# An early fetch of the first four tiles, an early split of the first weights, and all one-hot rows on VectorE

## The reference, cut to what matters

```python
logits = xf @ gate_w + gate_b
top_val, top_idx = jax.lax.top_k(logits, 2)
gate_score = jax.nn.softmax(top_val, axis=-1)
...
h = jax.nn.gelu(xf @ w1 + b1, approximate=False)
out = out + (h @ w2 + b2) * w[:, None]        # for each of the 8 experts
```

## Time and profile before

| what | value |
|---|---|
| time, median of 3 runs | 334.94 us (334.84 to 337.4) |
| time of the profiled execution | 337.69 us |
| its span in the profile | 336.0 us |
| busy: PE / PEld / DVE / ACT / POOL | 265.2 / 247.2 / 210.0 / 168.6 / 169.0 us |
| PE MATMUL L566 (fc1), x1872 | 154.5 us |
| PE MATMUL L582 (fc2), x936 | 150.7 us |
| POOL L1246 (one-hot rows), x32 | 32.0 us, mean 1010 ns |
| DVE L1130 (weights_lo), x16 | 36.7 us, mean 2293 ns |
| ACT L718 (weights_hi), x16 | 30.6 us, mean 1911 ns |
| chain that ended last | DMA 52%, issue 16%, PE 12%, DVE 9%, POOL 3%, ACT 3% |

### The profile page before, as it was taken

One profiled execution on the slowest core, in us unless ns is written; L12 is line 12 of the kernel. 1 busy time (PEld: TensorE's weight loads), 2 busy tenths in 40 slices (PEclk: granted clock), 3 DMA queues, 4 the chain that ended last, 5 costly groups with the idle time before them and its releaser, 6 DMA issues.

```text
span 336.0 us, 9465 instructions
## 1 busy us (share of the span) xinstructions
PE 265.2 (79%) x3109; PEld 247.2 (74%) x3109; DVE 210.0 (63%) x635; ACT 168.6 (50%) x465; POOL 169.0 (50%) x134
## 2 busy tenths in 40 slices
PE   3999952423014999999999999999999999999930
PEld 3998842312014989989999999998999999989920
DVE  5996689888963776766567656675575444443400
ACT  2042582463042886566756676567554544444410
POOL 5211106878952066666475657475636645463430
PEclk9985555555555999999999999999999999999995
DMA  6999999621114124454444444344434473435220
GB/s 183 352 375 377 376 376 375 234 95 64 64 44 100 19 34 70 77 90 72 82 69 79 67 80 75 73 69 77 78 69 67 80 97 66 77 58 78 28 22 14
DMA packets 47696, 40.17 MB, mean 120 GB/s; under 512 B 24113, under 2 KB 44354, under 8 KB 47650
## 3 DMA queue, kind: packets, MB, share of 16 engines
q1 hardware_dynamic: 39520, 28.85, 29.1%
q0 software_dynamic: 7488, 10.39, 20.3%
q10 hardware_dynamic: 642, 0.33, 0.4%
HBM read 25.07 MB, written 9.37 MB: 103 GB/s over the span
## 4 chain that ended last, share of the span: by engine, by line
DMA 52%; issue 16%; PE 12%; DVE 9%; POOL 3%; ACT 3%; DVEq 0%; ACTq 0%; POOLq 0%
DMA out_dram<-xn,add_at 50%; PE bank L421 4%; POOL wreg L1246 3%; PE bank L407 2%; DMA xs<-in_x_dram 1%; ACT wreg L718 1%; ACT xn L695 1%; DVE rows L944 1%; PE bank L449 1%; DVE wreg L1130 1%; DVE earlier L984 1%; PE bank L440 1%; DVE xs L921 1%; PE bank L485 1%; PE bank L464 1%
## 5 line engine op out<-in xcount | busy, mean ns | idle before, releaser
L566 PE MATMUL bank<-xTp,wreg 128*128 128x128 f16 x1872 | 154.5, 221 | 12.8 <-DVE wreg L1130 10.3
L582 PE MATMUL bank<-wreg,rows 128*128 x936 | 150.7, 273 | 0.0
L566 PEld LDWEIGHTS bank<-xTp,wreg 128*128 x1872 | 130.3, 99 | 21.8 <-issue 14.8
L782 ACT ACTIVATE rows<-bank,maskbias 128x128 f32<-128x128 f32 x312 | 88.6, 367 | 85.9 <-PE bank L566 36.5
L1274 POOL DMA_INDIRECT out_dram<-xn,add_at x39 | 78.4, 2011 | 92.1 <-ACT xn L792 61.1
L582 PEld LDWEIGHTS bank<-wreg,rows 128*128 128x128 f16 x936 | 80.7, 98 | 4.3
L1196 DVE TENSOR_SCALAR rows<-rows 128x512 f16<-128x512 f32 x78 | 33.8, 433 | 65.3 <-ACT rows L782 65.3
L1198 DVE SCALAR_TENSOR_TENSOR rows<-rows 128x512 f16<-128x512 f32 x78 | 54.0, 692 | 2.7
L1266 POOL DMA_INDIRECT xs<-xrows,fetch_at x39 | 45.4, 1165 | 18.0 <-issue 11.3
L1130 DVE SCALAR_TENSOR_TENSOR wreg<-wreg x16 | 36.7, 2293 | 19.7 <-ACT wreg L718 16.7
L718 ACT ACTIVATE wreg<-wreg x16 | 30.6, 1911 | 18.2 <-issue 14.5
(11 more groups left out here) (184 smaller groups left out, 209.8 us busy)
## 6 DMA issues: line engine op xcount, KB each, us to landing
wreg<-in_L_ffn_fc_w_dram SPq DMA_DIRECT2D x16, 1024.0 KB, 12.7
xrows<-rows SPq DMA_DIRECT2D x4, 528.0 KB, 3.0
xs<-in_x_dram SPq DMA_DIRECT2D x4, 512.0 KB, 8.5
out_dram<-xs SPq DMA_DIRECT2D x4, 512.0 KB, 8.6
xs<-xrows,fetch_at POOLq DMA_INDIRECT x39
xTp<-xs SPq DMA_TRANSPOSE x39
out_dram<-xn,add_at POOLq DMA_INDIRECT x39, 4.4
ctx_sb<-in_ctx_dram SPq DMA_DIRECT2D x1, 512.0 KB, 8.4
```

Source lines behind the costliest of these rows:

```text
L566: mm = pe.matmul(put, w, xT[:, i % NX, x_part, k, :], start=(k == 0 and n == 0), stop=(k == KC - 1 and n == 2))
L582: mm = pe.matmul(yb, h, w, start=False, stop=(c == FC - 1 and n == 2))
L782: op = act.activation(h32[i % 2][:, f * P:(f + 1) * P], bank[2 * (i % 2) + half][:, c * P:(c + 1) * P], ACT.Gelu, bias=b1cur[:, i % NX, f: ...
```

## The change

What it does, part by part:

1. One-hot rows: `at_col` and `at_rank` are both made on VectorE, as 16 `tensor_scalar` operations of 128 columns for each group, from an fp16 copy of the iota. GpSimd makes none. The rows move out of the spare weight region: one buffer of their own for groups 0 to 2, and a part of `xn` for group 3.
2. `row_low(3)` stands ahead of `slots(3)`; `norm1(3)` moves behind `add_attention(0)`.
3. `weights_hi(0)` waits on ACT for `units_ready` and the loads, and no longer for the token table. The cast of the token table moves from VectorE to ACT, behind `weights_hi(0)`.
4. The first expert always has four tiles; their columns, expert and regions are computed by themselves right behind `table_units` (`first_tiles`), PE makes a first fetch matmul from them, and VectorE copies the rows (`first_fetch`). Then come `weights_lo(0)`, `table_tiles`, `fetch(0)`, `weights_lo(1)` and `table_adds`.
5. PE makes a second fetch matmul ahead of the main loop. For tiles 0 to 3 it loads three registers from small tables; it waits for the full table at tile 4. It waits for unit 2r ahead of fc1 and for unit 2r+1 ahead of fc2 of an expert's first tile.

The diff, cut to its core:

```diff
-        spare = whalf[:, NU, :].rearrange("p (a b j q) -> p a b j q", a=2, b=2, j=GT * 2)
-        at_rank, at_col = spare[:, 0, :, :, :], spare[:, 1, :, :, :]
+        last_rows = xn[:, (NG - 2) % 2, :, :].rearrange("p t d -> p (t d)").bitcast(F16).rearrange("p (a j q) -> p a j q", a=2, j=GT * 2)
+        at_rank = [sb("at_rank", [P, GT * 2, P], F16)] * (NG - 1) + [last_rows[:, 0, :, :]]
+        at_col = [sb("at_col", [P, GT * 2, P], F16)] * (NG - 1) + [last_rows[:, 1, :, :]]
...
             pe.wait_ge(tokens_sb, 1)
             pe.wait_ge(cols_ready, 1)
-            pe.matmul(bank[0][:, 0:TILES], tokens_at[:, :], is_col[:, :], start=True, stop=True).then_inc(fetch_ps, 1)
-
-            pe.wait_ge(table_ready, 1)
-            pe.wait_ge(fetch_ready, 1)
+            pe.matmul(bank[6][:, 0:PER_RANK], tokens_at[:, :], is_col[:, 0:PER_RANK], start=True, stop=True).then_inc(fetch_ps, 1)
+            pe.wait_ge(cols_ready, 2)
+            pe.matmul(bank[6][:, 0:TILES], tokens_at[:, :], is_col[:, :], start=True, stop=True).then_inc(fetch_ps, 1)
+
...
                 if c == 0:
                     pe.wait_ge(xT_in[i % NX], (i // NX + 1) * 16)
+                    if i == 0 or unit_for(i) != unit_for(i - 1):
+                        pe.wait_ge(w_lo, unit_for(i) + 1)
...
+                if c == 0 and (i == 0 or unit_for(i) != unit_for(i - 1)):
+                    pe.wait_ge(w_lo, unit_for(i) + 2)
...
             def regions(i, n):
+                if i == 0:
+                    pe.wait_ge(first_ready, 1)
...
+                    return [(at[0], at[1], e) for j in range(n)]
+                if i == PER_RANK:
+                    pe.wait_ge(table_ready, 1)
...
+            weights_hi(0, unit_regions(0))
             act.wait_ge(tokens_ps, NG)
-            weights_hi(0, unit_regions(0))
+            act.activation(tokens_at[:, :], bank[1][:, 0:P], ACT.Copy).then_inc(tokens_sb, 1)
             at = unit_regions(1)
...
-                v.tensor_tensor(at_rank[:, g % 2, :, :], iota[:, :].unsqueeze(1).to_broadcast([P, GT * 2, P]),
-                                place_f[:, g, 1, :].unsqueeze(2).to_broadcast([P, GT * 2, P]),
-                                ALU.is_equal).then_inc(at_rank_ready, 1)
+
+            def onehot_rows(g):
+                if 1 <= g < NG - 1:
+                    v.wait_ge(tokens_ps, g)
+                if g == NG - 1:
+                    v.wait_ge(row_ready, g)
+                for j in range(GT * 2):
+                    n = g * GT + j // 2
+                    v.tensor_scalar(at_rank[g][:, j, :], iota_h[:, :], place_f[:, g, 1, j:j + 1], None, ALU.is_equal)
+                    op = v.tensor_scalar(at_col[g][:, j, :], iota_h[:, :], place_f[:, g, 0, j:j + 1], token[:, n:n + 1],
+                                         ALU.is_equal, ALU.mult)
+                op.then_inc(onehots, 1)
...
+            def first_tiles():
+                v.tensor_scalar(col_first[:, :], order_f[:, 0:1], float(RANKS // 2), None, ALU.mult).then_inc(vec_step, 1)
+                v.tensor_scalar(te_first[:, :], order_f[0:1, 0:1], 0.5, None, ALU.mult).then_inc(vec_step, 1)
+                v.tensor_copy(tw_first[:, 1:2], order_f[0:1, 0:1]).then_inc(vec_step, 1)
+                v.wait_ge(vec_step, done.up(3))
+                v.sem_inc(first_ready, 1)
+                v.tensor_scalar(is_col[:, 0:PER_RANK], iota_t[:, 0:PER_RANK], col_first[:, 0:1], iota_p[:, 0:1],
+                                ALU.add, ALU.is_equal).then_inc(cols_ready, 1)
+
+            def first_fetch():
+                v.wait_ge(fetch_ps, 1)
+                v.tensor_copy(fetch_at[:, 0:PER_RANK], bank[6][:, 0:PER_RANK]).then_inc(fetch_ready, 1)
...
             shift(3)
             route(3)
+            row_low(3)
             slots(3)
-            row_low(3)
+            onehot_rows(3)
             table_units()
+            first_tiles()
+            first_fetch()
+            weights_lo(0, unit_regions(0))
             table_tiles()
-            weights_lo(0, unit_regions(0))
-            table_adds()
-            weights_lo(1, unit_regions(1))
...
             fetch(0)
+            weights_lo(1, unit_regions(1))
+            table_adds()
             for i in range(TILES):
...
-            def onehot_rows(g):
-                pool.wait_ge(slots_ready, g + 1)
...
-                    op = pool.tensor_scalar(at_col[:, g % 2, j, :], iota[:, :], place_f[:, g, 0, j:j + 1], token[:, n:n + 1],
-                                            ALU.is_equal, ALU.mult)
-                op.then_inc(onehots, 1)
```

More of the change, by code:

```diff
@@ L61, in flamingo_block @@
     assert KC == 2 and HALVES == 2 and D == 256 and NG == 4 and FC == 8 and TILES == 39
-    assert GT == 2 * HALVES and 2 * NS == P and B == 2 * NG and NU < CODE and E * RANKS == P
+    assert GT == 2 * HALVES and 2 * NS == P and B == 2 * NG and NU < CODE and NXG == PER_RANK and (2 * T // E - 1) // P + 1 >= PER_RANK and E * RANKS == P
     xt = x.rearrange("b (h p) d -> p (b h) d", p=P)
@@ L125, in flamingo_block @@
         iota64 = iota[:, 0:NS]
+        iota_h = sb("iota_h", [P, P], F16)
         token = sb("token", [P, NT])
@@ L220, in flamingo_block @@
         te_i = sb("te_i", [1, TILES], I32)
+        te_first = sb("te_first", [1, 1], I32)
+        tw_first = sb("tw_first", [1, 2], I32)
+        col_first = sb("col_first", [P, 1])
         tw_i = sb("tw_i", [1, TILES, 2], I32)
@@ L310, in flamingo_block @@
         cols_ready = sem("cols_ready")
+        first_ready = sem("first_ready")
         fetch_ps = sem("fetch_ps")
@@ L336, in flamingo_block, with unit_for @@
             units_of_tile[(r - 1) * PER_RANK] = (2 * r + 1,)
-        def units_for(i):
-            return min(2 * (i // PER_RANK + 1), NU)
+        def unit_for(i):
+            return min(2 * (i // PER_RANK), NU - 2)
         block = stack.enter_context(nc.Block())
@@ L525, in token_table @@
                 pe.wait_ge(onehots, g + 1)
-                pe.wait_ge(at_rank_ready, g + 1)
                 for j in range(GT * 2):
-                    mm = pe.matmul(bank[1][:, 0:P], at_col[:, g % 2, j, :], at_rank[:, g % 2, j, :],
+                    mm = pe.matmul(bank[1][:, 0:P], at_col[g][:, j, :], at_rank[g][:, j, :],
                                    start=(g == 0 and j == 0), stop=(g == NG - 1 and j == GT * 2 - 1))
@@ L586, in regions @@
             def regions(i, n):
+                if i == 0:
+                    pe.wait_ge(first_ready, 1)
+                    at = nc.values_load_multi_w_load_instructions(
+                        tw_first[0:1, :], engines=[mybir.EngineType.PE], min_val=0, max_val=NU,
+                        skip_runtime_bounds_check_because="regions NU and 2e + 1 of an expert")[1]
+                    e = nc.values_load_multi_w_load_instructions(
+                        te_first[0:1, :], engines=[mybir.EngineType.PE], min_val=0, max_val=E - 1,
+                        skip_runtime_bounds_check_because="an expert")[1][0]
+                    return [(at[0], at[1], e) for j in range(n)]
+                if i == PER_RANK:
+                    pe.wait_ge(table_ready, 1)
                 at = nc.values_load_multi_w_load_instructions(
@@ L828, in _ @@
             v.memset(units_i[:, 0:1], NU).then_inc(vec_step, 1)
+            v.memset(tw_first[:, 0:1], NU).then_inc(vec_step, 1)
             v.wait_ge(pool_const, 2)
             v.tensor_copy(iota[:, :], iota_i[:, :]).then_inc(vec_step, 1)
+            v.tensor_copy(iota_h[:, :], iota_i[:, :]).then_inc(vec_step, 1)
             v.tensor_copy(token[:, :], iota_ki[:, :]).then_inc(vec_step, 1)
@@ L1108, in table_tiles @@
                 v.tensor_single_scalar(te_i[:, :], code_i[:, :], 5, op=ALU.logical_shift_right).then_inc(vec_step, 1)
-                v.wait_ge(fetch_ps, 1)
-                v.tensor_copy(fetch_at[:, :], bank[0][:, 0:TILES]).then_inc(fetch_ready, 1)
+                v.wait_ge(fetch_ps, 2)
+                v.tensor_copy(fetch_at[:, PER_RANK:TILES], bank[6][:, PER_RANK:TILES]).then_inc(fetch_ready, 1)
                 v.wait_ge(vec_step, done.up(2))
@@ L1138, in _ @@
             pick_sets(1)
-            norm1(3)
             weigh_sets(1)
             add_attention(0)
+            norm1(3)
             pick_sets(2)
@@ L1152, in _ @@
             slots(0)
+            onehot_rows(0)
             row_low(0)
@@ L1160, in _ @@
             slots(1)
+            onehot_rows(1)
             row_low(1)
@@ L1170, in _ @@
             slots(2)
+            onehot_rows(2)
             row_low(2)
@@ L1282, in _ @@
                 fetch_rows(i)
+            pool.wait_ge(fetch_ready, 2)
             pool.wait_ge(add_at_ready, 1)
```

18 lines of the change are left out of this document (3 added, 15 removed).

## The result

| | time, median of 4 runs (range) | profiled execution | its span |
|---|---|---|---|
| before | 334.94 us (334.84 to 337.4) | 337.69 us | 336.0 us |
| after | 341.24 us (338.7 to 342.21) | 342.21 us | 340.2 us |

The ratio of after to before is 1.0163, interval 1.011 to 1.0216: slower, by 3.7 to 7.2 us. Medians, here and in the experiments, are of all runs; the ratios leave out the few runs that the record marks as slow. The forecast was 339.0 us, +4.1 on the median before (a ratio of 1.012), in a range of 333.5 to 342.8.

What follows compares the result with a forecast made beforehand. PE was taken to bound the 39 tiles, so only its entry into the loop counts: PE's start +3.7 us, first fc2 +4.1, never taken back. Added to the median before, that gave 339.0 us, range 333.5 to 342.8.

Steps and rivals of the forecast that it cites:

- What bounds it: Main loop: PE bounds the 39 tiles, waiting only 2.5 us, so what decides is when PE gets in.
- Part 1, the pitch: One-hot rows on VectorE: 0.18 us each start to start, bounds 0.13 and 0.24; +5.19 over three groups.
- The credit for GpSimd's silence: Groups 1 to 3 on VectorE: without GpSimd's rows disturbing it, VectorE gains 1.25 us.
- Part 2: Moves: row_low(3) fills a 0.8 us wait and pushes slots(3) back 0.4; norm1(3) costs nothing, 0.2 at most.
- Part 3, ACT's order: ACT before first_fetch: the token table's cast stands behind weights_hi(0), so the early fetch is 3 us late, at 97.9.
- Part 4, the queue behind the new wait: VectorE stands still 3.4 us in first_fetch, its remaining list behind it; PE starts at 108.7, +3.7; fc2 at 115.3, +4.1.
- in the same cold clock: PE between first fc1 and fc2: the 72 matmuls take 6.19 us as before, reaching fc2 at 114.9.
- the 0.4 that I had for the split: First fc2: PE is there at 114.9 but waits for VectorE's split, so fc2 starts at 115.3.
- Cheap rows: Rival at the 64 one-hot operations: issued every 0.08 to 0.11 us; 333.9 us at 0.10, down to 331.2; chance 0.18.
- Dear rows: Rival at the one-hot rows: pitch 0.23 to 0.25 us, shift +7.3 to +8.6, 342.2 to 343.5 us; chance 0.15.
- The loop takes it back: Rival in the main loop: slack in GpSimd's output adds eats half the shift, 337.0 us; chance 0.1.
- The early start is one: Rival at first_fetch: ACT's cast slips ahead or VectorE's wait is short; 3.4 us less, +0.7, 335.6 us; chance 0.07.

Runs made afterwards that it cites:

- fp32_rows: Kernel after with its one-hot rows made from the fp32 iota instead of the fp16 copy; 344.5 us in one execution.
- norm_back: Kernel after with norm1(3) put back ahead of weigh_sets(1); 341.27 us, ratio 1.0112 to the kernel before.
- rows_only: Kernel before with only the one-hot rows moved to VectorE from the fp16 iota, in the old two buffers; 343.15 us, ratio 1.0128.
- cast_first: Kernel after with ACT's cast of the token table ahead of weights_hi(0); 339.21 us, ratio 1.0055 to the kernel before.
- tables_first: Kernel after with ACT's cast ahead of weights_hi(0) and table_tiles ahead of weights_lo(0); 338.68 us in one execution.
- early_start: cols_and_cast with PE's second fetch behind tile 0, table_tiles behind fetch(0), remaining tables behind tile 0's splits, and earlier register loads; 332.85 us, ratio 0.9886.
- cols_and_cast: The edits of cols_on_gpsimd and cast_first together in the kernel after; 335.64 us, ratio 0.9986 to the kernel before.
- cols_on_gpsimd: Kernel after with at_col rows of groups 0 to 2 back on GpSimd and their at_rank one VectorE operation per group; 336.93 us, ratio 1.0003.

## Why the prediction was right

**What bounds it** held. The loop is full in both kernels, and the change acts only by when PE gets into it: after the first fc2 225 us were forecast and 226.1 came. (The view behind the earlier trace rows also has the 10.3 us wait that ends at 105.00; the 2.5 us are those behind it.)

**Part 1, the pitch**, was the term that carried the sum and held: 0.18 forecast, 0.193 measured, inside the bounds of 0.13 and 0.24. Over 64 operations that is 0.8 us more than forecast. It lay near the middle because of the rows that looked most like it, two fp32 operations with per-partition scalars; fp32_rows found just their 0.20 again. The split of it (a scalar costs up to 0.06, half the bytes 0.035) agrees with the 0.055 and 0.033 found, as far as the 0.055 is the scalar's.

**The credit for GpSimd's silence**, 1.25 us, came out at about 1.4. **Part 2:** `norm1(3)` moves for nothing, as norm_back showed. `row_low(3)` ahead of `slots(3)` was to earn 1.13 - 0.4 = 0.73 us at `table_units`; rows_only, which leaves it in its old place, has that mark at 41.82 and the kernel after at 41.09. The two differ in where the rows are stored too, so this agrees, but does not show it alone.

**Part 3, ACT's order.** `first_fetch` was forecast 3 us late because the cast stands behind `weights_hi(0)`. VectorE stood idle for 3.22 us (3.4 forecast), and cast_first took the idle time away by moving that one operation.

**Part 4, the queue behind the new wait.** The steps were right one by one: `weights_lo(0)` 1.83 us after the copy (1.55 forecast), PE held by the second fetch matmul until `table_tiles` is through, fc1 at 58.81 (58.16). The 0.65 between them is there already at `table_units` (41.09 for 40.43) and fits the pitch: 0.8, less the 0.15 by which the credit was too small.

**The step that failed** is the last one, "in the same cold clock". I took the 72 matmuls of before, 6.19 us, and had VectorE's split come last at fc2. In the kernel after they take 7.02 us. The stretches of PE (columns as above), before and after:

```profile
107.00:108.00 1.00, 1.00 (x12) 1.00 (x11) 0.00 (x0) 0.17 (x1) 0.00 (x0) 0.50 0.48 135
108.00:109.00 1.00, 1.00 (x15) 1.00 (x13) 0.00 (x0) 0.97 (x4) 0.00 (x0) 0.68 0.00 0
```

```profile
111.50:112.00 0.50, 0.50 (x8) 0.50 (x6) 0.00 (x0) 0.00 (x0) 0.00 (x0) 0.50 0.00 0
112.00:112.50 0.50, 0.50 (x8) 0.50 (x6) 0.47 (x3) 0.09 (x1) 0.28 (x1) 0.52 0.00 0
112.50:113.00 0.50, 0.50 (x12) 0.50 (x11) 0.47 (x2) 0.50 (x3) 0.50 (x1) 1.00 0.12 33
```

Before, the granted clock goes from 1.2 to 2.4 GHz about 3.6 us after fc1 starts at 105.00; after, about 5.4 us after 107.09. That is 0.83 us more for the same matmuls, and the split, ready at 113.40, is no longer last. So the shift at fc2 is 5.18 and not 4.1: 0.65 from the late start, 0.83 from the clock, less the 0.4 that I had for the split. In tables_first, where PE took 5.9 us for them (106.00 to 111.93), the split does bind. Why the clock rose later is open. Over the ten kernels the same 72 matmuls took 5.9 to 7.2 us, and the clock rose 2.8 to 5.8 us after the first of them, each seen in one execution. norm_back has 7.1, fp32_rows, with PE's code unchanged, 6.3. So the 0.83 may be a draw of the execution and not the change's doing, and a forecast should give this term about a microsecond.

**The rivals.** Cheap rows: out, no row came under 0.165 us (its lowest shift, -3.7, comes to -3.6 or -3.9 by the prediction's own credits; nothing hangs on it). Dear rows: out for fp16, but what it described is fp32_rows. The loop takes it back: out, the loop gave 1.3 us more. The early start is one: out as the change stands; it takes the moves of early_start, on top of cols_and_cast, and then there is one.

What stays open: the time after is 6.3 above the first median of before, and 4.4 to 4.7 above the medians of before that stood beside the experiments. The marks give +5.2 at the first fc2, and 6.5 with the 1.3 of the loop. Whether the 2.3 us wait for a transpose at 140 us belongs to the change was not tried.

## What to carry to other kernels

When two engines work side by side, moving work from the one with idle time to the full one costs its whole price less the disturbance; price small operations by their start-to-start pitch in the trace, with as many per-partition scalars as they will have. An early fetch brings nothing as long as something that needs the late tables stands ahead of its consumer in an in-order queue: follow each engine's written order from the new result to its user, and move what is in between. After each mend ask again what is last: here it was VectorE's rows, then ACT's cast, then PE's second fetch, then the gather.

## What was not expected of the hardware

**The front phase does not take the same time twice.** PE's stretch from 24 to 34 us (columns as above) in the kernels before, after and cast_first:

```profile
24.00:34.00 10.00, 9.46 (x47) 8.81 (x46) 7.17 (x34) 3.07 (x10) 1.01 (x1) 0.50 1.06 378
```

```profile
24.00:34.00 10.00, 9.46 (x47) 8.81 (x48) 8.43 (x45) 3.58 (x13) 1.01 (x1) 0.50 1.06 377
```

```profile
24.00:34.00 10.00, 8.45 (x74) 7.87 (x74) 8.99 (x47) 5.57 (x22) 1.76 (x2) 1.00 1.06 377
```

The first two do 47 matmuls at 1.2 GHz, the third 74 at 2.4 GHz, with the same code on PE. T0 is 45.28 us there, and 48.3 to 50.5 in all others.

These rows do not tell the kernels before and after apart. What does is earlier, the same eight matmuls on PE, before and then after:

```profile
17.07 1.91 PE L500 MATMUL bank<-ident,ctx_sb 128*128 128x128 f32 x8
```

```profile
16.88 1.06 PE L505 MATMUL bank<-ident,ctx_sb 128*128 128x128 f32 x8
```

They take 1.91 us and 1.06, while the granted clock reads full in both kernels from 2 to 22 us: here that column does not tell how fast PE works. Beside the 45.28 of cast_first, T0 has two groups: 48.28 to 48.55 (after, norm_back, cols_on_gpsimd, cols_and_cast) and 50.09 to 50.54 (before and the other four). Kernels with the same code up to T0 stand in both, so the difference is the execution's and not the change's. It moves T0 by up to 5 us, more than the cast was worth, and one profiled execution shows one draw of it. What sets it no run shows.

**A gather takes longer on GpSimd beside a weight split.** GpSimd in the kernel after:

```profile
96.94 1.23 POOL L1297 DMA_INDIRECT xs<-xrows,fetch_at  x1 [22.24 <-DVE fetch_at L1106]
98.47 2.33 POOL L1297 DMA_INDIRECT xs<-xrows,fetch_at  x1 [0.30 <-issue]
101.11 1.04 POOL L1297 DMA_INDIRECT xs<-xrows,fetch_at  x1 [0.30 <-issue]
```

The second gather starts inside the `weights_lo(0)` of 97.67 to 99.96 and takes 2.33 us; it ends 0.84 after the split does. The first one starts before the split and is not longer. GpSimd in the kernel before has the same beside its split of 97.64 to 99.93:

```profile
97.54 0.96 POOL L1266 DMA_INDIRECT xs<-xrows,fetch_at  x1 [0.30 <-issue]
98.81 1.94 POOL L1266 DMA_INDIRECT xs<-xrows,fetch_at  x1 [0.31 <-issue]
```

That gather ends at 100.75, 0.82 after the split, and early_start has one that ends 0.84 after its own (94.02 + 2.29 against 93.18 + 2.29). In the ten kernels 11 gathers start inside a split, 0.05 to 1.20 us behind its start. They last 1.91 to 3.07 us, and each ends 0.81 to 0.86 us after the split; none of the 379 others lasts over 1.52. The output adds do likewise: all 123 that start inside a split end 1.61 to 1.68 us after it. So an indirect DMA that starts on GpSimd while the split is running seems to do its work only after it. The Trainium skill, page "SBUF — State Buffer", section "Who interferes with whom", tells of a pair of ports that VectorE and GpSimd share, and infers that `tensor_tensor`, which takes only the read side of it, leaves the making of descriptors alone. The split is a `scalar_tensor_tensor`, also with two inputs from SBUF, and for it the rows speak against that, though no run took the overlap away.
